# Attention block on one core: the value product in fp16, and the value projection moved between the keys and the output product

## The reference

```python
x = x + tanh(g_xattn) * attention(layernorm(x), ctx, ctx)   # 16 heads of 64, causal mask
x = x + tanh(g_ffn) * ffn(layernorm(x))                     # quantised, 768 wide
# attention:
qh, kh, vh = heads(q @ Wq), heads(k @ Wk), heads(v @ Wv)    # Wq, Wk, Wv: 256 x 1024
dots = einsum('bhid,bhjd->bhij', qh, kh) * 64 ** -0.5       # masked
out = einsum('bhij,bhjd->bhid', softmax(dots), vh)          # the value product
return out @ Wo + bo
```

## Time and profile before

| what | us |
|---|---|
| median of 3 runs (1622.98 to 1626.07) | 1624.89 |
| the profiled execution | 1626.47 |
| its span, first to last instruction | 1624.6 |
| PE busy | 1530.6 (94%) |
| DVE busy | 1385.1 (85%) |
| ACT busy | 1253.4 (77%) |
| POOL busy | 1033.8 (64%) |

### The profile page before, as it was taken

One profiled execution on the slowest core, in us unless ns is written; L12 is line 12 of the kernel. 1 busy time (PEld: TensorE's weight loads), 2 busy tenths in 40 slices (PEclk: granted clock), 3 DMA queues, 4 the chain that ended last, 5 costly groups with the idle time before them and its releaser, 6 DMA issues. The chain is left out here.

```text
span 1624.6 us, 38058 instructions
## 1 busy us (share of the span) xinstructions
PE 1530.6 (94%) x12556; PEld 1251.8 (77%) x12556; DVE 1385.1 (85%) x2247; ACT 1253.4 (77%) x3222; POOL 1033.8 (64%) x1004
## 2 busy tenths in 40 slices
PE   7899999999999999999999999789989997995998
PEld 5787887877877878878778788677767776775887
DVE  7888888888888888888888889878887998998996
ACT  5887887888778778878887787566758998885674
POOL 3988988888888889888888888600006664740000
PEclk9999999999999999999999999999998999997999
DMA  6554445444444544454444445369957884755664
GB/s 195 118 127 103 105 106 122 104 92 115 106 105 103 126 102 105 107 121 104 92 115 106 105 103 98 86 205 344 321 215 262 282 287 153 276 227 187 218 214 145
DMA packets 347365, 252.23 MB, mean 155 GB/s; under 512 B 287792, under 2 KB 317616, under 8 KB 344368
## 3 DMA queue, kind: packets, MB, share of 16 engines
q1 hardware_dynamic: 347312, 251.58, 55.1%
HBM read 105.25 MB, written 76.02 MB: 112 GB/s over the span
## 5 line engine op out<-in xcount | busy, mean ns | idle before, releaser
L496 ACT ACTIVATE prob<-masked,neg_max 128x128 f32<-128x128 f32 x1024 | 397.6, 391 | 35.1 <-DVE neg_max L662 31.6
L431 POOL TENSOR_TENSOR prob_parts<-prob,prob_parts 128x512 f16<-128x512 f32 x254 | 310.3, 1241 | 2.7 <-ACT prob_parts L504 1.6
L426 POOL TENSOR_TENSOR prob<-prob,scaled 128x512 f32<-128x512 f32 x256 | 271.6, 1061 | 20.1
L660 DVE TENSOR_TENSOR masked<-score,mask_add 128x512 f32<-128x512 f32 x256 | 174.6, 682 | 74.0 <-PE score L963 67.9
L504 ACT ACTIVATE prob_parts<-prob 128x512 f16<-128x512 f32 x254 | 159.0, 627 | 75.6 <-POOL prob L426 71.7
L496 ACT ACTIVATION_READ_ACCUMULATOR prob<-masked,neg_max 128x1 f32 x1024 | 193.3, 189 | 0.0
L662 DVE TENSOR_REDUCE neg_max<-masked 128x4 f32<-128x512 f32 x256 | 175.6, 686 | 8.8
L438 POOL TENSOR_TENSOR probT<-turn 128x512 f32<-128x512 f16 x125 | 173.2, 1386 | 0.0
L1723 POOL TENSOR_SCALAR xThi<-n_x 128x1024 fp32r<-128x1024 int16 x15 | 43.8, 2919 | 202.9 <-DMA n_x<-n_x_d 166.8
L976 PE MATMUL y<-wo_hi,o_hi 128*128 128x256 f32 x508 | 148.3, 292 | 15.9 <-DVE o_lo L667 15.2
L424 POOL TENSOR_TENSOR scaled<-rsums,pscale 128x4 f32<-128x4 f32 x256 | 66.4, 259 | 124.0 <-DVE rsums L654 123.9
(11 more groups left out here) (249 smaller groups left out, 4485.5 us busy)
## 6 DMA issues: line engine op xcount, KB each, us to landing
gate<-gate_d SPq DMA_DIRECT2D x30, 768.0 KB, 4.3
n_x<-n_x_d SPq DMA_DIRECT2D x25, 512.0 KB, 4.9
gate_d<-stage SPq DMA_DIRECT2D x8, 1536.0 KB, 5.5
n_u_d<-w_raw SPq DMA_DIRECT2D x16, 768.0 KB, 4.1
stage<-n_u_d SPq DMA_DIRECT2D x16, 768.0 KB, 6.0
gate_d<-gate SPq DMA_DIRECT2D x7, 1536.0 KB, 5.5
x_in<-in_x SPq DMA_DIRECT2D x16, 512.0 KB, 3.9
ctx_in<-in_ctx_columns SPq DMA_DIRECT2D x16, 512.0 KB, 4.8
```

The source lines that it names most:

```text
L426: gp.tensor_tensor(prob[:, h], prob[:, h], scaled[:, h, :].rearrange("p (b o) -> p b o", o=1).broadcast_to([P, NB, P]), ALU.mult).then_inc ...
L431: gp.tensor_tensor(prob_parts[:, h, 1], prob[:, h].rearrange("p b k -> p (b k)"), prob_parts[:, h, 0], ALU.subtract).then_inc(prob_low, 1)
L496: nc.scalar.activation(prob[:, h, b, :], masked[:, h, b, :], ACT.Exp, bias=neg_max[:, h, b:b + 1], accum_out=psums[:, h, b:b + 1]).then_in ...
L660: nc.vector.tensor_tensor(masked[:, h], score[h][:], mask_add[:], ALU.add).then_inc(masked_done, 1)
```

## The change

The value product takes fp16 operands. Each value becomes a high and a low fp16 part (`v16`), in a unit `v_unit` chosen so that no value leaves fp16's range: a bound from the largest weights and the largest context, by a product of one column on TensorE (`value_bound`). The probabilities' two fp16 parts are used as they come out of the transposes. The joins go. In their place stand three products for each old one: high by high, high by low, low by high. The unit is multiplied back in the residual (`y_unit`).

ScalarE takes the high part of every value projection (`values_high`), VectorE the low part (`values`). TensorE has the value projections directly behind the keys. Besides, the copy of the keys moves ahead of the exponentials in steps 0 to 2 of group 0, GpSimd's bias addition moves from step 6 to step 0 of the next group, and the last unit's probabilities are split instead of copied.

```diff
@@ SP, GpSimd
             def turn_prob(u, h):
                 sp.wait_ge(prob_low, 2 * u + h + 1)
-                wait(sp, probT_copied[h], u - 1)
+                wait(sp, pv_done, u - 1)
...
             def step(g, c):
                 u, new, soft, old, more = parts(g, c)
-                if old:
-                    join_second(u - 3, (c + 1) % 2, NC // 2 * g + (c - 1) // 2)
...
-                if c == 6 and new:
-                    gp.wait_ge(xres_loaded, 16 * (g + 1))
...
+                if c == 0 and not (isinstance(g, int) and g == 0):
+                    add_bias(g - 1)
@@ ScalarE
+            def values_high(g, i, n):
+                b, before = nth(g, i)
+                if n == 0:
+                    act.wait_ge(v_scaled, 4 * g + 3)
+                act.wait_ge(projected[b], before + 1)
+                nc.scalar.activation(v16[:, n % NB, n // NB, 0], proj[b][:], ACT.Copy, scale=v_mul[:, 0:1]).then_inc(v_high, 1)
...
+                early = isinstance(g, int) and g == 0 and c < 3
+                vs = jobs_of(c, "v") if new else []
+                if early and c == 0:
+                    w_high_part(3)
+                if early:
+                    copy_k(g, c, u)
...
                 if soft:
                     exps(u - 1, 0)
-                if new:
+                if new and not early:
                     copy_k(g, c, u)
+                for i, n in vs[:1]:
+                    values_high(g, i, n)
...
                 if soft:
                     exps(u - 1, 1)
...
+                for i, n in vs[1:]:
+                    values_high(g, i, n)
@@ VectorE
-            def values(g, c):
-                for i, n in jobs_of(c, "v"):
+            def values(g, jobs):
+                for i, n in jobs:
                     b, before = nth(g, i)
-                    dve.wait_ge(projected[b], before + 1)
-                    nc.vector.tensor_copy(v_sb[:, n % NB, 0:VH], proj[b][:]).then_inc(copied[b], 1)
+                    dve.wait_ge(v_high, NC * g + n + 1)
+                    nc.vector.scalar_tensor_tensor(v16[:, n % NB, n // NB, 1], proj[b][:], v_mul[:, 0:1], v16[:, n % NB, n // NB, 0],
+                                                   ALU.mult, ALU.subtract).then_inc(copied[b], 1)
+
+            def ctx_top(g):
+
+                dve.wait_ge(ctx_loaded, 16 * (g + 1))
+                nc.vector.tensor_reduce(c_top[:], ctx_in[:], X, ALU.max, apply_absolute_value=True).then_inc(v_scaled, 1)
+
+            def value_scale(g):
+
+                dve.wait_ge(v_bound, g + 1)
+                nc.vector.tensor_scalar(v_unit[:], trans[:, 0, 0:1], 1.0 / VMAX, VTINY, ALU.mult, ALU.max).then_inc(v_scaled, 1)
+                dve.wait_ge(v_scaled, 4 * g + 2)
+                nc.vector.reciprocal(v_mul[:], v_unit[:]).then_inc(v_scaled, 1)
...
@@ VectorE, ahead of the steps
             w_low_part(2)
+            dve.wait_ge(w_loaded[5], 16)
+            nc.vector.tensor_reduce(w_top[:], w_stage(2), X, ALU.max, apply_absolute_value=True)
+            ctx_top(0)
             w_low_part(3)
@@ TensorE
                 for b in range(NB):
...
-                    for h in range(2):
-                        last = nc.tensor.matmul(pv[h * HD:(h + 1) * HD, b, :], v_sb[:, b, c * P + h * HD:c * P + (h + 1) * HD],
-                                                probT[:, h, b, :], start=True, stop=True)
+                    for n, (m, t) in enumerate(((0, 0), (0, 1), (1, 0))):
+                        for h in range(2):
+                            at = c % NB * P + h * HD
+                            last = nc.tensor.matmul(pv[h * HD:(h + 1) * HD, b, :], v16[:, b, c // NB, m, at:at + HD],
+                                                    turn[:, slot, h, t * NB + b, :], start=(n == 0), stop=(n == 2))
...
+            def value_bound(g):
+
+                pe.wait_ge(v_scaled, 4 * g + 1)
+                for k in range(KC):
+                    last = nc.tensor.matmul(trans[:, 0, 0:1], c_top[:, k:k + 1].broadcast_to([P, P]), w_top[:, k:k + 1],
+                                            start=(k == 0), stop=(k == KC - 1))
...
+                if first:
+                    value_bound(0)
                 if nxt:
                     transpose_in(g, *ts[0])
+                if first or fourth:
+                    pe.wait_ge(w_ready, 3 if first else 6)
+                if new:
+                    for i, n in jobs_of(c, "v"):
+                        value(g, i, n)
                 if oldest:
...
                     out_product(u - 4, (c - 4) % NC)
                 if nxt:
                     transpose_in(g, *ts[1])
...
-                if new:
-                    for i, n in jobs_of(c, "v"):
-                        value(g, i, n)
+                    value_bound(g + 1)
                 if old:
-                    times_v(u - 3, co, (g, c, u) if new else None)
+                    times_v(u - 3, co, (c + 1) % 2, NC // 2 * g + (c - 1) // 2, (g, c, u) if new else None)
```

More of the change, by code:

```diff
@@ L41 @@
 PSCALE = 32768.0
+VMAX = 60000.0
+VTINY = 1e-30
 def split(hi, lo):
@@ L202, in attention @@
         xres_loaded = sem("xres_loaded")
-        probT_copied = [sem(f"probT_copied{h}") for h in range(2)]
+        v_high = sem("v_high")
+        v_scaled = sem("v_scaled")
+        v_bound = sem("v_bound")
+        last_turned = sem("last_turned")
         pv_done = sem("pv_done")
@@ L449, in step @@
                         make_rstd2(g - 1)
-                if c == 6 and new:
-                    gp.wait_ge(xres_loaded, 16 * (g + 1))
-                    gp.tensor_tensor(xres[:], xres[:], bo_g[:].rearrange("p (o n) -> p o n", o=1).broadcast_to([P, NB, D]),
-                                     ALU.add).then_inc(xres_ready, 1)
+                if c == 0 and not (isinstance(g, int) and g == 0):
+                    add_bias(g - 1)
+                if c == 6 and new and not more:
+                    add_bias(g)
                 if soft:
@@ L532, in step @@
                     exps(u - 1, 1)
-                if isinstance(g, int) and g == 0 and c < 3:
+                if early and c < 2:
                     w_high_part(4 + c)
-                if new and c > 2:
-                    for i, n in jobs_of(c, "v"):
-                        b, before = nth(g, i)
-                        act.wait_ge(projected[b], before + 1)
-                        nc.scalar.activation(v_sb[:, n % NB, VH:2 * VH], proj[b][:], ACT.Copy).then_inc(copied[b], 1)
+                for i, n in vs[1:]:
+                    values_high(g, i, n)
                 if soft:
@@ L573, in _ @@
             attended(U - 2)
-            act.wait_ge(last_step, 1)
             act.wait_ge(pv_done, U - 1)
-            nc.scalar.activation(probT[:, 0], trans[:], ACT.Copy).then_inc(probT_copied[0], 1)
-            for n in range(4):
+            for h in range(2):
+                act.wait_ge(last_step, h + 1)
+                nc.scalar.activation(turn[:, 1, h, 0:NB], trans[:], ACT.Copy).then_inc(v_high, 1)
+                if h == 0:
+                    ffn_high_part(0)
+            for n in range(1, 4):
                 ffn_high_part(n)
@@ L642, in w_low_half @@
                     last.then_inc(w_ready, 1)
-            def join_prob(u, h, slot, times):
-                dve.wait_ge(prob_turned[h][slot], 16 * times)
-                wait(dve, pv_done, u)
-                nc.vector.tensor_tensor(probT[:, h], turn[:, slot, h, 0:NB], turn[:, slot, h, NB:2 * NB],
-                                        ALU.add).then_inc(probT_copied[h], 1)
             def reciprocals(u, h):
@@ L711, in step @@
                     second_stats(g - 1)
+                if c == 4:
+                    output_unit(g)
+                if c == 6 and more:
+                    ctx_top(g + 1)
                 if c == 5 and after_first:
@@ L723, in step @@
                         work(*args)
+                if isinstance(g, int) and u == 0:
+                    value_scale(0)
+                vs = jobs_of(c, "v")
+                if new:
+                    values(g, vs[:1])
                 if soft:
                     reciprocals(u - 1, 1)
-                if c < 3:
-                    values(g, c)
+                if new:
+                    values(g, vs[1:])
+                if nxt:
+                    value_scale(g + 1)
                 if c == 4 and after_first:
@@ L868, in _ @@
             second_moments(G - 1)
[L869 to L870 removed]
+            second_max(G - 2).then_inc(last_step, 1)
+            dve.wait_ge(last_step, 5)
             second_norm(G - 1, 0, NB)
@@ L937, in scores_free, with times_v @@
                     wait(pe, masked_done, 2 * (u - 1) + h + 1)
-            def times_v(u, c, then=None):
+            def times_v(u, c, slot, times, then=None):
                 for h in range(2):
-                    pe.wait_ge(probT_copied[h], u + 1)
+                    if times is None:
+                        pe.wait_ge(last_turned, 2)
+                    else:
```

(1 more changed line is left out.)

73 lines of the change are left out of this document (35 added, 38 removed).

## The result

| | median us | runs | ratio to before, 95% interval |
|---|---|---|---|
| before | 1624.50 | 1622.98 to 1626.07 | |
| after | 1653.39 | 1651.53 to 1658.02 | 1.0182 [1.0158, 1.0206] |

The kernel became slower by 28.9 us. The forecast was 1631 with a range that ended at 1650: the sign was right, the size was not. The profiled execution took 1658.02 us, with a span of 1656.2; it is the slowest of the four runs, and the next table, which compares it with the profiled execution of before (1626.47), adds up to 30.7 us instead of 28.9.

What follows compares the result with a forecast made beforehand. TensorE bounds the kernel (68.84 of 70 us busy), with VectorE and ScalarE trailing little in eight-step passes. Fourteen passes at +0.3 give +4, start +3, end -1: +6, so 1632.5 us profiled, 1631 median; range 1610 to 1650.

Steps and rivals of the forecast that it cites:

- Value product: In each step on TensorE: twelve fp16 pairs at 0.057 us take 0.83 instead of 1.03, a gain of 0.19.
- that rival: Weight loads lie open on TensorE: value product 1.97 us, +0.94 a step, kernel some 1735 us; chance 0.04.
- The round: Steps 4 to 0 of each pass, across all four engines: queries of step 1 at 534.8 against 534.08, +0.7 us.
- the 0.38 saved in steps 1 and 2: TensorE in steps 1 and 2, where VectorE and ScalarE wait for it: gain 0.19 us each, -0.38 a pass.
- Normalising 2.1 (515.25 to 517.35): maxima of step 7 at 518.3: VectorE in step 6: normalising takes 2.1 us, so the maxima of step 7 start 0.95 us later than before.
- So step 7 absorbs most of the delay: Step 7: exponentials at 519.7 against 519.55 before, when GpSimd's bias addition held up the query copy.
- Start: Kernel start: weight maxima and bound move the values from 17.24 to 19.7, low parts queue on VectorE; +3 us.
- End: Kernel end: two joins of 2.73 us ahead of the last maxima go, the last two transposes take longer; -1 us.
- 0.6 more each: Last two transposes at the kernel's end: a high and a low copy in a row, 0.6 us more each.
- TensorE alone decides: VectorE and ScalarE have more slack: a pass saves 2.5 us, kernel 1592 us; chance 0.2, alone or in part.

Runs made afterwards that it cites:

- e9: Changed kernel plus one wait: in step 6 GpSimd starts the probabilities' low parts only after VectorE's normalising; 1643.84 us, ratio 1.0094 to before.
- e1: Changed kernel with VectorE's normalising moved from step 6 to steps 3 and 4; 1632.54 us, ratio 1.0041 to before.
- e4: Changed kernel with the maximum over the context moved from step 6 to the end of step 2; 1651.70 us, ratio 1.0154 to before.
- e6: Changed kernel with VectorE's residual of step 3 moved behind the low half and second reciprocals; 1639.93 us, ratio 1.0082 to before.
- e3: Changed kernel with the start reordered on VectorE and ScalarE, and 36 unread transposes keeping TensorE busy ahead of the bound; 1652.69 us, ratio 1.0160 to before.
- e8: Changed kernel with the edits of e1, e3, e4, e6 and e7 together; 1587.72 us, ratio 0.9751 to before.
- e12: Kernel of e7 plus twelve unread transposes in step 7, where TensorE stood idle; 1629.10 us, ratio 1.0015 to before.
- e7: Changed kernel with ScalarE's query copies earlier in steps 4 to 7 and 0, and the key copy earlier in step 0; 1651.93 us, ratio 1.0156 to before.
- e11: Changed kernel with the values back behind the output product, high halves still ahead of the second exponentials; 1717.50 us, ratio 1.0564 to before.

## Why the prediction was right, and where it was wrong

**Value product: right, undersized.** 0.29 a step instead of 0.19, since a pair costs less than 0.057 (twelve in 0.79 us with start and end). The loads, 110 ns each in the mean and 24 in those 0.79 us (one after the other they would be 2.64), do not lie open, and that rival falls.

**The round: right but for one term.** Measured from the queries of step 1 (470.27 in the forecast's clock, 487.72 in the trace), the forecast less the 0.38 saved in steps 1 and 2:

| from the queries of step 1 | forecast | after | row |
|---|---|---|---|
| query copy of step 4 | 25.05 | 24.79 | ACT 512.51 |
| maxima of step 5 | 32.55 | 32.39 | DVE 520.11 |
| query copy of step 6 | 40.35 | 40.39 | ACT 528.11 |
| second reciprocals of step 6 | 45.55 | 45.71 | DVE 533.43 |
| maxima of step 7 | 47.65 | 48.65 | DVE 536.37 |
| query copy of step 0 | 56.85 | 57.84 | ACT 545.56 |
| second value product of step 0 | 59.60 | 60.61 | PE 548.33 |
| queries of the next step 1 | 64.15 | 65.20 | PE 552.92 |

Within 0.3 everywhere up to step 6, then 1.0 late to the end. A part of this agreement is luck: the first three steps were 0.26 shorter than forecast, where the product cost less, and from the query copy of step 4 to that of step 6 it took 15.60 instead of 15.30. The step that failed reads "Normalising 2.1 (515.25 to 517.35): maxima of step 7 at 518.3". The price was a row's, and it held what GpSimd had done beside it in the kernel before; the change moved GpSimd's bias addition away and with it, as the two traces read, the gap through which the fourth instruction had slipped. It measured 2.94, 0.85 more; the rest of the 1.0 is 0.16 from before it. "So step 7 absorbs most of the delay" fell with it: the exponentials of step 7 are bound by these maxima. Fourteen passes of 1.39 instead of 0.3 are 15 us of the 23 that the forecast lacks. e9 takes only the holding away and gets back 0.83 of the 1.09 a pass; e1 takes all of the normalising out of step 6 and gets back 1.59.

**Start: undersized.** +3 was forecast, 9.1 were lost in the profiled execution, 7.5 to 8.1 in e4, e6 and e9. The values were to start at 19.7; they start at 21.47, since the weights landed later (their maximum starts at 17.13, not 15.9) and the bound of one column took 0.87 instead of 0.5. Then they ran at a granted clock of 0.50 (21.47 to 26.87), 5.4 us for twelve instead of 2.9. No term of the sum had TensorE's clock in it. By e3 some of this is swallowed later anyway.

**End: wrong sign.** -1 was forecast, +1.7 measured from the first scores of group 15 on; up to its last scores that group gives back 1.6, and what follows them loses 3.3. "0.6 more each" for the last transposes: TensorE stands 2.97 us idle ahead of the second, behind the split of the first one's result, against 1.28 before, and the output product behind it starts every 0.21 us, at a granted clock of 0.50 (1079.0 to 1081.5). So does the one behind the last scores (0.51 from 1065 to 1068), behind a wait of 3.19. Here too no term had the clock in it.

**The rivals.** "TensorE alone decides" was refuted for this change, and is what e8 comes to: 1592 was its price, 1587.7 the measurement. That they are so near is luck: e8 has five edits that the forecast did not have, and its passes save 2.9, not 2.5.

## What to carry to other kernels

A duration taken from a row may hold only beside the same neighbours: where a change shifts what GpSimd does, a VectorE instruction such as this normalising is to be priced with and without a GpSimd instruction beside it (0.4, or 1.13 to 1.26 us, here), and the schedule chosen so that the two don't meet on the path. Work for TensorE that is ready while it waits (values here) is worth trying there: in e12 twelve products that nobody reads kept the granted clock of step 7 at 1.00, where e7 had 0.85, and the pass fell from 64.90 to 63.55. In a round of four engines a single repair can show nothing (e7) because something else swallows it, here the clock; so look for what swallowed it, and try repairs together before dropping any.

## What the runs showed of the hardware that was not expected

The granted clock fell behind short waits too: to 0.55 in the stretch from 535.00 to 537.50 in e7, behind two waits of 0.87 and 1.19 us in one step. The same waits did not do it every time: 0.85 and 1.19 left it at 1.00 in the eleventh pass of e7, and 2.45 did in eight of fourteen passes of e11. With 0.20 and 1.19 (after) and with 0.28 and 0.42 and transposes between (e12) it stayed at 1.00 in every pass. What decides in the other cases is not shown. Not all of VectorE's work was held by GpSimd: the maximum over 1024 columns at 530.54 took 1.19 us beside a multiplication on GpSimd (530.98 to 532.02), and 1.21 at the start of the kernel (19.34), where GpSimd was idle, while a multiplication and addition on 128x4 elements (L621, step 4, 518.04) took 1.03 beside one, and 0.16 at the start of the kernel, where GpSimd was idle.
